# Row maxima of causal scores: diagonal blocks taken by ScalarE and GpSimd instead of a masked pass of VectorE

## The chip, the core and the metric

The kernel runs on one core of a Trainium2 chip. The metric is the device time of one execution in microseconds (us), the median of several runs. Engines are named as in the profile: PE is TensorE (PEld its weight loads), DVE is VectorE, ACT is ScalarE, POOL is GpSimd, SP is SyncE, which only issues DMAs here.

## The reference

One layer of a transformer with modulated norms, for 8 sequences ("batches" below) of 1024 tokens with 256 features, 16 heads of 16 dimensions:

```python
h = _layernorm(x) * (1 + ca) + sa
x = x + ga * attention(h)        # 16 heads, causal, softmax over keys
h = _layernorm(x) * (1 + cb) + sb
x = x + gb * (shared_ffn(h) + routed_ffn(h))   # 8 experts, the top 2 of each token
...
scores = jnp.einsum('...hqd,...hkd->...hqk', q, k) / np.sqrt(d_model)
scores = jnp.where(causal, scores, -1e+30)
attn = jax.nn.softmax(scores, axis=-1)
```

## The kernel before

**Work and stages.** The 16 heads of a batch are taken in four groups of four heads. For each group the kernel first finds, for every query and head, the largest allowed score (the "maxima"). That number goes as two extra rows into the query operand, so that the second computation of the scores, with keys on the partitions, comes out of the matmul with its maximum already taken off, and ACT can apply the exponential as it stands. The maxima of a group are computed one group ahead of their use.

**Slots.** A batch has 80 slots (`SLOTS`), 20 a group (`GROUP`). In slot t PE computes one unit of scores into a bank (`scores`, L1804), ACT takes the exponential of it out of the bank into one of `RING` = 8 probability buffers in SBUF (`exps`, L1076), POOL zeroes the triangle of a unit on the diagonal (`select`, L890), and PE multiplies the probabilities of slot t - 4 (`LAG`) with the values (`values`, L1827). Into the same slots tables of numbers lay the rest of the work: the projections of the next batch (`qk`, `v`, `turn`), and for the batch before it the output projection, the second norm, the router and the shared feed-forward network (`up` L1841, `down` L1893, with ACT's L1098 and L1109, DVE's L1310, L1320 and L1328, POOL's L959). The first batch has instead the splitting of the weights (`share`). After the last batch follow the tiles of the experts.

**Maxima.** In the first 14 slots of a group (`MAX_SLOTS`) PE also computes 18 chunks of scores of the next group: `MAX_CHUNKS` lists nine, and each is done for both pairs of heads (`PAIRS`). A chunk fills one bank, 128 queries by 1024: 512 keys of each of the two heads of a pair (`s`). Its entries `(qt, k0, nk, at)` say which block of 128 queries, which keys, and where in the bank. The two heads lie on different partitions of the operands, so their matmuls (L1780) run beside each other. DVE reads the bank:

```python
if p % NCH not in MASKED:
    vec.tensor_reduce(max_part[:, :, i, col:col + 1].rearrange("p s n -> p (s n)"), of, AX.X, ALU.max).then_inc(max_read, 1)
...
        last = vec.tensor_tensor_reduce(scored, scored, mask[:, 512 - nk:], scale=1.0, scalar=NEG, op0=ALU.add, op1=ALU.max,
                                        accum_out=max_part[:, s, i, to:to + 1])
```

Four of the nine chunks lie wholly below the diagonal or have no piece that ends at it: one reduce (L1273). The five others (`MASKED`) hold a piece that ends with a block on the diagonal, and each of their pieces (eight in all, on two sides) is one instruction that adds the mask and takes the maximum (L1279, in the profile CUSTOM_DVE_ANT_0) and one that reads the accumulator (DVE_READ_ACCUMULATOR2_ANT, L1279 too). `shifts` (L1289 to L1292) then folds the partial maxima, and a turn on PE (`max_turn`, L1791), a copy on ACT (L1059) and two DMAs (L677) bring them into the query operand.

**Banks and order.** PSUM has three banks of 1024 columns (`BUFFERS`) that serve all of this in turn; two further ones take the value products. `WORK` is one list of steps, and every engine goes through it in that order with its own share of each step. Which bank a step takes is planned when the program is built (`buffers`): the one that is free first by the tables `BUSY` and `READ`, with `READ_MASKED` = 20 for a masked chunk and 18 for a plain one. PE waits (`take`, `was_read`) until the last user of that bank has been read. The expert weights of the tail are loaded over the query and key operands and the first probability buffers when these are done (`fetch`, L690).

**At the start** the 18 chunks of group 0 are computed and read one after the other, with nothing else beside them.

Of the kernel before, what the change touches and what calls it, by code (L numbers as in the profile page):

```python
# [14 lines left out]
P = 128  # L15
# [34 lines left out]
RING = 8  # L50
# [6 lines left out]
SEG = {0: 0, 2: 1, 1: 2, 5: 3, 6: 4, 4: 5, 3: 6, 7: 7}  # L57
MAX_CHUNKS = (
    (((3, 0, 512, 0),), 24),
    (((7, 0, 512, 0),), 28),  # L60
    (((7, 512, 512, 0),), 29),
    (((5, 0, 512, 0),), 14),
    (((0, 0, 128, 0), (2, 0, 384, 128)), 3),
    (((6, 0, 512, 0),), 16),
    (((1, 0, 256, 0), (5, 512, 256, 256)), 10),
    (((4, 0, 512, 0),), 21),
    (((6, 512, 384, 0), (4, 512, 128, 384)), 17),
)
NCH = len(MAX_CHUNKS)
MASKED = [i for i, (pieces, _) in enumerate(MAX_CHUNKS) if any(k0 + nk == (qt + 1) * P for qt, k0, nk, _ in pieces)]  # L70
MAXES = PAIRS * NCH

# [167 lines left out]
def work(v):  # L240

    units, tail, spill, head = BODY[v]
    out = []
    for t in range(SLOTS if units else LAG + 2):
# [12 lines left out]
        if not units:  # L257
            continue
        extra = [("normalise", 0)] if t == NORMALISE_AT else []
# [9 lines left out]

        readers = ("rest", "place", "low", "lengths")  # L270
# [66 lines left out]
READ_MASKED = 20  # L337
# [9 lines left out]
def buffers(v, was):  # L347
# [3 lines left out]
    for kind, *at in WORK[v]:  # L351
# [14 lines left out]
        if kind in RINGED and kind not in READER and (kind not in PARTS_OF or at[1] == PARTS_OF[kind] - 1):  # L366
            free[took[use]] = now + (READ_MASKED if kind == "max" and at[1] % NCH in MASKED else READ[kind])
            closed.add(use)
# [15 lines left out]
POOL_SET = 15 + 2 * NE  # L384


def adaln_layer(nc, x, w_qk, w_v, w_o, ffn_w, router_w, bias, c_t, w_mod, out):
# [15 lines left out]
    with ExitStack() as ctx:  # L403
# [9 lines left out]
        arena = sb("arena", [P, 2 * NG * PAIRS * T + RING * 2 * GH * QC], F16)  # L413
# [20 lines left out]
        mask = sb("mask", [P, 512], BF16)  # L434
        ident = sb("ident", [P, P], F32)
        ident_b = sb("ident_b", [P, P], F16)
        max_part = sb("max_part", [P, 2, PAIRS, 4 * NT], F32)
# [37 lines left out]
        probs = flat.rearrange("p (r n) -> p r n", r=RING)  # L475
# [38 lines left out]
        late = flat[:, RING // 2 * GH * QC:]  # L514
# [49 lines left out]
        max_full, max_read, max_ready, max_turned = sem("max_full"), sem("max_read"), sem("max_ready"), sem("max_turned")  # L564
        rows_ready, shift_in = sem("rows_ready"), sem("shift_in")
# [44 lines left out]
        def at_max(b, g, p):  # L610
            return b * (NG * MAXES) + (g * MAXES + p + 1)

# [38 lines left out]
        def _(sp):  # L651
# [31 lines left out]
            def fetch(e):  # L683
# [4 lines left out]
                if g >= NG:  # L688
                    sp.wait_ge(values_done, at_unit(B - 1, SLOTS - 1 - RING // 2))
# [171 lines left out]
        def _(pool):  # L861
            gp = nc.gpsimd
            gp.memset(ident[:, :], 0.0).then_inc(pool_set, 1)
            gp.memset(mask[:, :], 0.0).then_inc(pool_set, 1)
# [1198 lines left out]
```

## Time and profile before

| what | us |
|---|---|
| three runs | 2168.48, 2179.09, 2185.64 |
| median | 2179.09 |
| profiled execution, span from first to last instruction | 2187.9 |

The profiled execution is one of its own, and its span is the only time known of it. Its instructions' durations are what the prediction counts with. The profile page gives busy time by engine; a window of the trace gives the same for a stretch of time; the chain of waits goes back from the last instruction to what released each step.

### The profile page before, as it was taken

How to read it: one execution, taken by the hardware profiler on the slowest of the kernel's cores; microseconds unless marked ns; L12 is line 12 of the kernel's file. 1: busy time of each engine (PE TensorE's matmuls, PEld its weight loads, DVE VectorE, ACT ScalarE, POOL GpSimd, SP SyncE). 2: the span in 40 equal slices, each digit the busy share in tenths (PEclk: the TensorE clock that was granted, in tenths of full speed). 3: DMA queues.
4: the chain of work that ended last, by engine and by line, in shares of the span. 5: the costliest groups of instructions: out<-in, count | busy, mean ns of one | idle time of the engine just before them, and what ended most of it. 6: DMA issues, size and time to landing. Idle time of an engine off the chain costs nothing.

```text
span 2187.9 us, 47736 instructions
## 1 busy us (share of the span) xinstructions
PE 1958.7 (90%) x17942; PEld 1036.3 (47%) x17942; DVE 1634.5 (75%) x4447; ACT 1085.8 (50%) x1417; POOL 830.9 (38%) x825
## 2 busy tenths in 40 slices
PE   5778889899999989999999999999998988999995
PEld 2223334344444444444443434343434577788773
DVE  7887788777877788778878877878787376655575
ACT  1556445554555455545554555455554545444431
POOL 1121133234323432343233333333232357876653
PEclk7688879999999999999999999999998999999998
DMA  3346220201111201120211020211100446797696
GB/s 125 94 169 192 89 64 16 59 22 46 45 38 43 71 20 47 37 70 16 65 30 62 22 65 22 71 30 53 49 26 25 158 88 113 133 170 123 153 285 201
DMA packets 109663, 175.67 MB, mean 80 GB/s; under 512 B 14576, under 2 KB 80376, under 8 KB 108288
## 3 DMA queue, kind: packets, MB, share of 16 engines
q1 hardware_dynamic: 82656, 136.37, 20.9%
q0 software_dynamic: 26592, 36.00, 9.1%
q8 instruction: 149, 2.44, 0.5%
q14 instruction: 74, 0.61, 0.1%
q10 hardware_dynamic: 192, 0.26, 0.1%
HBM read 76.43 MB, written 70.44 MB: 67 GB/s over the span
## 4 chain that ended last, share of the span: by engine, by line
PE 55%; DVE 29%; ACT 5%; issue 4%; DMA 3%; POOL 2%; SPq 2%; POOLq 0%; ACTq 0%; DVEq 0%
PE bank L1841 11%; DVE bank L1279 8%; PE bank L1893 8%; DVE max_part L1273 8%; PE bank L1873 6%; PE bank L1804 5%; PE misc L1827 5%; PE bank L1780 4%; PE pv L1827 3%; PE bank L1754 3%; PE bank L1884 2%; PE bank L1920 2%; ACT arena L1076 2%; PE bank L1742 1%; DVE max_part L1279 1%
## 5 line engine op out<-in xcount | busy, mean ns | idle before, releaser
L1076 ACT ACTIVATE arena<-bank 128x1024 f32<-128x1024 f32 (+1 forms) x640 | 593.2, 935 | 422.7 <-PE bank L1804 419.1
L1279 DVE CUSTOM_DVE_ANT_0 bank<-bank,mask 128x512 f32<-128x512 f32 (+3 forms) x1024 | 472.2, 521 | 65.8 <-PE bank L1780 62.4
L890 POOL TENSOR_SCALAR_AFFINE_SELECT arena<-arena 128x512 f32<-128x512 f32 x256 | 170.3, 672 | 651.0 <-ACT arena L1076 650.4
L1841 PE MATMUL bank<-feat_parts,ffn_sb 128*128 128x512 f16 x1536 | 367.4, 388 | 8.8 <-DVE max_part L1279 4.9
L1273 DVE TENSOR_REDUCE max_part<-bank 128x2 f32<-128x1024 f32 x256 | 312.4, 1220 | 28.2 <-PE bank L1780 26.2
L1804 PE MATMUL bank<-arena 50*128 50x256 f16 (+1 forms) x2560 | 246.3, 272 | 68.7 <-DVE max_part L1273 22.7
L1780 PE MATMUL bank<-arena 48*128 48x512 f16 (+3 forms) x1536 | 234.1, 350 | 56.7 <-DVE max_part L1279 20.8
L953 POOL DMA_INDIRECT sum<-arena,feat x142 | 231.9, 1633 | 138.1 <-issue 67.0
L959 POOL TENSOR_TENSOR hidden<-silu_h,hidden 128x512 f16<-128x512 f32 x128 | 155.8, 1220 | 234.0 <-ACT hidden L1109 233.4
L1827 PE MATMUL misc<-arena,v_sb 128*32 128x256 f32 (+1 forms) x3072 | 239.8, 386 | 1.9 <-POOL arena L890 1.9
L1841 PEld LDWEIGHTS bank<-feat_parts,ffn_sb 128*128 128x128 f16 x1536 | 141.5, 99 | 197.8 <-issue 33.1
L1873 PE MATMUL bank<-parts,arena 128*128 128x256 f16 x1704 | 201.0, 275 | 13.7 <-DVE arena L1493 11.4
L1893 PE MATMUL bank<-ffn_sb,hidden 128*128 128x256 f16 x1536 | 182.4, 276 | 21.7 <-POOL hidden L959 12.5
L1804 PEld LDWEIGHTS bank<-arena 50*128 50x128 f16 x2560 | 82.6, 96 | 246.0 <-issue 82.0
L1873 PEld LDWEIGHTS bank<-parts,arena 128*128 x1704 | 161.8, 98 | 41.1 <-issue 16.3
L1780 PEld LDWEIGHTS bank<-arena 48*128 48x128 f16 x1536 | 60.5, 95 | 245.0 <-issue 95.6
L1893 PEld LDWEIGHTS bank<-ffn_sb,hidden 128*128 128x128 f16 x1536 | 147.2, 99 | 57.1 <-issue 23.5
L1827 PE MATMUL pv<-arena,v_sb 128*32 128x256 f32 (+1 forms) x2048 | 159.2, 385 | 0.0
L1098 ACT ACTIVATE silu_h<-bank 128x512 f32<-128x512 f32 x112 | 66.9, 597 | 162.5 <-PE bank L1841 162.3
L1279 DVE DVE_READ_ACCUMULATOR2_ANT max_part<- 128x1 f32 x1024 | 145.3, 142 | 0.0
L935 POOL DMA_INDIRECT lists<-rows,slot_now x128 | 127.6, 997 | 34.9 <-issue 32.4
L1493 DVE SCALAR_TENSOR_TENSOR arena<-bank,arena 128x512 f32<-128x512 f32 x71 | 49.0, 690 | 119.1 <-ACT arena L1132 119.0
(218 smaller groups left out, 2477.2 us busy)
## 6 DMA issues: line engine op xcount, KB each, us to landing
arena<-parts SPq DMA_DIRECT2D x380, 64.0 KB, 2.3
feat<-lists SPq DMA_DIRECT2D x71, 265.0 KB
sum<-feat_parts SPq DMA_DIRECT2D x9, 1024.0 KB, 6.1
rows<-x SPq DMA_DIRECT2D x8, 1024.0 KB, 5.5
x_sb<-x SPq DMA_DIRECT2D x16, 512.0 KB, 5.6
sum<-norm SPq DMA_DIRECT2D x14, 512.0 KB, 3.3
ffn_parts<-hidden SPq DMA_DIRECT2D x8, 768.0 KB, 4.1
arena<-ffn_parts SPq DMA_DIRECT2D x8, 768.0 KB, 6.7
```

The costliest lines, as they stand in the source:

```text
L890: gp.affine_select(p, p, [[0, GH], [1, P]], ALU.is_ge, 0.0, 0, -1).then_inc(masked, 1)
L953: gp.indirect_dma_start(sum_dram[i % 2], bass.IndirectOffsetOnAxis(ap=tile_id[i % 8][:, t:t + 1], axis=0), tile_out[i % 4][:, t, :], None, ...
L959: gp.tensor_tensor(hidden[:, 1, k % 8, :], silu_h[:, k % 2, :], hidden[:, 0, k % 8, :], ALU.subtract).then_inc(hidden_low, 1)
L1076: sc.activation(to[:, :, lo:QC], of[:, :, lo:QC], ACT.Exp, scale=SCALE / QK_SCALE ** 2).then_inc(exp_done, 1)
L1273: vec.tensor_reduce(max_part[:, :, i, col:col + 1].rearrange("p s n -> p (s n)"), of, AX.X, ALU.max).then_inc(max_read, 1)
L1279: last = vec.tensor_tensor_reduce(scored, scored, mask[:, 512 - nk:], scale=1.0, scalar=NEG, op0=ALU.add, op1=ALU.max, accum_out=max_part[ ...
L1780: last = mm(to[:, 512 * s + at:512 * s + at + nk], q_stack[r, g, i, qt * P:(qt + 1) * P], k_stack[r, g, i, k0:k0 + nk], start=True, stop=True)
L1804: last = mm(to[:, at + lo:at + QC], k_stack[r, g, i, kt * P:(kt + 1) * P], q_stack[r, g, i, QC * c + lo:QC * (c + 1)], start=True, stop=True)
L1827: last = mm(attended[n % 2][32 * j:32 * j + 32, lo:QC], v_sb[:, kt, h:h + 32], probs[:, u % RING, at + lo:at + QC], start=(kt == 0), stop= ...
L1841: last = mm(to[:, 512 * m:512 * m + 512], w_up[s][W_PART[i]][:, f, m * RH + h * P:m * RH + (h + 1) * P], feat_parts[:, A_PART[i], f, c * 5 ...
L1873: last = mm(to[:, 512 * h + ROWS * m:512 * h + ROWS * (m + 1)], weights(W_PART[x] * UW + f * 2 * RH + m * RH + h * P, P), tile_feat[i % 2] ...
L1893: last = mm(to[:, 0:D], hidden[:, A_PART[i], j, t * P:(t + 1) * P], w_down[j // 2][W_PART[i]][:, j % 2, :], start=(i == 0 and j == 0), sto ...
```

## The change

The masked pass is gone. `MAX_CHUNKS` is cut anew: each of the eight diagonal blocks of 128 by 128 is now a piece of its own, and the eight fill two chunks (`DIAG_AT` = 1 and 5 of nine). The seven other chunks need no mask and are read by one DVE reduce each, which gives one partial maximum for each run of 512, 256 or 128 keys (the last number of an entry); `max_part` has five places a query block in place of four (`KEPT`). A diagonal chunk is copied by ACT out of its bank into one of three copy buffers (`copy_max`), masked there by POOL one slot later (`select_max`), and reduced by DVE from SBUF two slots after that (`diag_max`). PE may write the bank again when ACT has copied it. The copy buffers are the last three of the eight probability buffers, of which five are left (`RING` = 5, `ARENA` = 8). In the bank plan a diagonal chunk counts 18 like a plain one. The load of an expert's weights over the probability buffers waits for the last use of just the buffers that it covers.

```diff
-RING = 8
+RING = 5
+ARENA = 8
...
+KEPT = 5
+SEG = {7: 0, 1: 1, 5: 2, 3: 3, 6: 4, 2: 5, 4: 6, 0: 7}
 MAX_CHUNKS = (
-    (((3, 0, 512, 0),), 24),
-    (((7, 0, 512, 0),), 28),
...
+    (((7, 0, 512, 0),), 0, 1, 512),
+    (((7, 896, 128, 0), (5, 640, 128, 128), (6, 768, 128, 256), (4, 512, 128, 384)), 1, 10, 128),
...
+    (((1, 128, 128, 0), (3, 384, 128, 128), (2, 256, 128, 256), (0, 0, 128, 384)), 9, 10, 128),
...
+DIAG_AT = (1, 5)
+OF_DIAG = [p % NCH in DIAG_AT for p in range(MAXES)]
+COPIES = 3
...
+        made[t + 1] += [("select_max", *e[1:]) for e in maxes if OF_DIAG[e[2]]]
+        made[t + 3] += [("diag_max", *e[1:]) for e in maxes if OF_DIAG[e[2]]]
...
-READ_MASKED = 20
+READ_MASKED = 18
...
-                    sp.wait_ge(values_done, at_unit(B - 1, SLOTS - 1 - RING // 2))
+                    used = ((e + 1) * 2 * UW - 2 * NG * PAIRS * T - 1) // (2 * GH * QC)
+                    sp.wait_ge(values_done, at_unit(B - 1, SLOTS - RING + used))
...
+            def select_max(b, g, p):
+                n = at_diag(b, g, p)
+                pool.wait_ge(diag_copied, n)
+                some = copy_of(p).rearrange("p (q n) -> p q n", n=P)
+                gp.affine_select(some, some, [[0, 2 * 4], [-1, P]], ALU.is_ge, NEG, 0, 1).then_inc(diag_masked, 1)
...
+            def copy_max(b, v, g, p):
+                n = at_diag(b, g, p)
+                if past(n - COPIES):
+                    act.wait_ge(diag_read, n - COPIES)
+                act.wait_ge(max_full, at_max(b, g, p))
+                sc.activation(copy_of(p), buffer_of(v, ("max", g, p))[:, :], ACT.Copy).then_inc(diag_copied, 1)
...
+            def kept(g, p, of):
+                pieces, col, step, nk = MAX_CHUNKS[p % NCH]
+                many = sum(x[2] for x in pieces) // nk
+                to = max_part[:, :, p // NCH, col:col + (many - 1) * step + 1:step]
+                return vec.tensor_reduce(to, of, AX.X, ALU.max)
...
+                kept(g, p, buffer_of(v, ("max", g, p))[:, :].rearrange("p (s q n) -> p s q n", s=2, n=nk)).then_inc(max_read, 1)
...
+            def diag_max(b, g, p):
+                dve.wait_ge(diag_masked, at_diag(b, g, p))
+                kept(g, p, copy_of(p).rearrange("p (s q n) -> p s q n", s=2, n=P)[:, :, :, 0:P]).then_inc(diag_read, 1)
...
-                    pe.wait_ge(max_read, at_max(b if at[0] else b + 1, *at))
+                    of = b if at[0] else b + 1
+                    if OF_DIAG[at[1]]:
+                        pe.wait_ge(diag_copied, at_diag(of, *at))
+                    else:
+                        pe.wait_ge(max_read, at_plain(of, *at))
```

The order of DVE's instructions in a group of the loop batch, third to sixth chunk, before (L1279 the masked pass, L1273 the reduce, L1300 and L1302 the normalising of outputs):

```order
L1273 TENSOR_REDUCE max_part<-bank0 128x2
L1279 ISA bank2,max_part<-bank2,mask 128x128
L1279 ISA max_part 128x1
L1279 ISA bank2,max_part<-bank2,mask 128x128
L1279 ISA max_part 128x1
L1279 ISA bank2,max_part<-bank2,mask 128x384
L1279 ISA max_part 128x1
L1279 ISA bank2,max_part<-bank2,mask 128x384
L1279 ISA max_part 128x1
L1300 RECIPROCAL l_inv<-misc 128x8
L1302 TENSOR_TENSOR o_tok<-misc,l_inv 128x2x64
L1273 TENSOR_REDUCE max_part<-bank0 128x2
```

And DVE at the same place after the change (L1312 is `kept`; 128x2x4 are eight partial maxima; arena is a copy buffer; L1351 and L1361 are the silu products):

```order
L1312 TENSOR_REDUCE max_part<-bank1 128x2x4
L1312 TENSOR_REDUCE max_part<-bank0 128x2
L1341 RECIPROCAL l_inv<-misc 128x8
L1343 TENSOR_TENSOR o_tok<-misc,l_inv 128x2x64
L1312 TENSOR_REDUCE max_part<-arena 128x2x4
L1351 SCALAR_TENSOR_TENSOR silu_h<-silu_h,bank0 128x512
L1361 SCALAR_TENSOR_TENSOR silu_h<-bank0,silu_h 128x512
L1312 TENSOR_REDUCE max_part<-bank1 128x2
```

Eight instructions for a chunk with two masked pieces have become one, and the reduce of a copy stands two slots behind the chunk's own place, ahead of that slot's silu products.

ACT at the same place before (L1076 the exponential, of half a unit where it says 4x128; L1066 the copy of an output):

```order
L1076 ACTIVATE arena<-bank0 128x4x128
L1076 ACTIVATE arena<-bank2 128x1024
L1076 ACTIVATE arena<-bank0 128x4x128
L1076 ACTIVATE arena<-bank0 128x1024
L1076 ACTIVATE arena<-bank2 128x1024
L1066 ACTIVATE o_raw<-misc 128x256
L1076 ACTIVATE arena<-bank1 128x1024
L1098 ACTIVATE silu_h<-bank1 128x512
```

And after it (L1112 the exponential, L1087 the copy of a diagonal chunk, L1102 the copy of an output, L1134 the silu's tanh):

```order
L1112 ACTIVATE arena<-bank0 128x4x128
L1087 ACTIVATE arena<-bank2 128x1024
L1112 ACTIVATE arena<-bank1 128x1024
L1112 ACTIVATE arena<-bank2 128x1024
L1102 ACTIVATE o_raw<-misc 128x256
L1112 ACTIVATE arena<-bank2 128x1024
L1087 ACTIVATE arena<-bank1 128x1024
L1134 ACTIVATE silu_h<-bank0 128x512
```

Each copy stands behind its own slot's exponential and ahead of the next one's.

PE in the first slots of such a group before (L1804 scores, L1827 value products, L1780 the chunks):

```order
L1780 MATMUL bank2<-arena 128x512 x2
L1804 MATMUL bank0<-arena 128x256 x4
L1827 MATMUL misc<-arena,v_sb 32x256 x4
L1780 MATMUL bank1<-arena 128x512 x2
L1804 MATMUL bank2<-arena 128x256 x4
L1827 MATMUL misc<-arena,v_sb 32x128 x4
L1780 MATMUL bank0<-arena 128x512 x2
```

And after it (L1855, L1878 and L1831 are the same three):

```order
L1831 MATMUL bank2<-arena 128x128 x8
L1855 MATMUL bank1<-arena 128x256 x4
L1878 MATMUL misc<-arena,v_sb 32x256 x4
L1831 MATMUL bank0<-arena 128x512 x2
L1855 MATMUL bank2<-arena 128x256 x4
L1878 MATMUL misc<-arena,v_sb 32x128 x4
L1831 MATMUL bank1<-arena 128x384 x2
```

The steps of PE keep their order; a diagonal chunk has eight matmuls of 128 columns for two of 512, and the banks fall differently.

## Rows read from the trace of the kernel before

**Rows 1.** Page: busy us by engine; PE in 40 slices, tenths.

```profile
PE 1958.7 (90%) x17942; PEld 1036.3 (47%) x17942; DVE 1634.5 (75%) x4447; ACT 1085.8 (50%) x1417; POOL 830.9 (38%) x825
...
PE   5778889899999989999999999999998988999995
```

**Rows 2.** Windows: length, then busy us of PE, PEld, DVE, ACT, POOL, clock, DMA.

```profile
50.00:260.00 210.00, 164.10 (x1482) 59.47 (x1484) 169.63 (x469) 117.97 (x134) 32.66 (x41) 0.79 0.43 142
1000.00:1213.00 213.00, 198.30 (x1852) 92.51 (x1850) 171.04 (x486) 113.19 (x149) 73.11 (x81) 0.98 0.15 44
```

**Rows 3.** Chain of waits, 1000 to 1213 us: shares by line.

```profile
by line: PE bank L1841 13.8%; PE bank L1893 10.3%; DVE max_part L1273 9.9%; DVE bank L1279 9.2%; PE bank L1804 6.4%; PE misc L1827 5.7%; PE bank L1780 5.1%; PE pv L1827 4.1%; PE bank L1920 3.3%; issue 3.1%; PE bank L1754 2.6%; ACT arena L10
```

**Rows 4.** Windows of stretches with maxima, columns as in rows 2.

```profile
940.00:976.00 36.00, 32.50 (x287) 11.73 (x286) 31.52 (x96) 17.28 (x25) 16.58 (x20) 0.91 0.19 61
1000.00:1029.00 29.00, 25.06 (x257) 11.78 (x254) 26.49 (x81) 17.57 (x22) 10.80 (x13) 1.00 0.01 2
1050.00:1093.00 43.00, 39.98 (x381) 17.41 (x379) 38.49 (x114) 21.56 (x30) 12.13 (x16) 1.00 0.18 47
1049.70:1055.30 5.60, 4.80 (x64) 1.62 (x62) 4.40 (x11) 4.49 (x7) 2.97 (x4) 1.00 0.38 97
```

**Rows 5.** Waits of PE, 1000 to 1213 us: total us, times, longest.

```profile
PE bank L1804 <- DVE silu_h L1320: 2.4, 2, 2.1
PE bank L1804 <- DVE max_part L1273: 2.1, 6, 0.4
PE bank L1893 <- ACT feat L1026: 1.4, 2, 0.8
PE bank L1780 <- DVE max_part L1273: 1.4, 4, 0.5
PE bank L1780 <- ACT arena L1076: 1.3, 4, 0.5
```

**Rows 6.** Same window, L1279 alone, then L1273 alone: DVE busy, clock, DMA.

```profile
1000.00:1213.00 213.00, 61.13 (x256) 0.98 0.15 44
...
1000.00:1213.00 213.00, 39.06 (x32) 0.98 0.15 44
```

**Rows 7.** Groups by form, three reduces of DVE: busy us, mean ns, idle before.

```profile
L1273 DVE TENSOR_REDUCE max_part<-bank 128x2 f32<-128x1024 f32 x256 | 312.4, 1220 | 28.2 <-PE bank L1780 26.2
...
L1484 DVE TENSOR_REDUCE feat<-feat 128x2 f32<-128x16 f32 x71 | 12.1, 170 | 2.4
...
L1289 DVE TENSOR_REDUCE max_row<-max_part 128x32 f32<-128x128 f32 x32 | 8.9, 278 | 0.3
```

**Rows 8.** Timeline of PE: start us, us, line, instruction.

```profile
1043.86 0.62 PE L1791 MATMUL bank<-ident_b,max_bf 128*8 128x128 f16 x8
...
1044.41 0.39 PE L1804 MATMUL bank<-arena 50*128 50x256 f16 x4
...
1050.57 0.39 PE L1780 MATMUL bank<-arena 48*128 48x512 f16 x2
...
1050.80 0.28 PE L1804 MATMUL bank<-arena 50*128 50x128 f16 x4
```

**Rows 9.** ACT's 1024-wide exponential; POOL's select of 512 and 128 elements.

```profile
L1076 ACT ACTIVATE arena<-bank 128x1024 f32<-128x1024 f32 x512 | 520.7, 1020 | 364.7 <-PE bank L1804 361.5 <-PE misc L1827 1.3
...
L890 POOL TENSOR_SCALAR_AFFINE_SELECT arena<-arena x256: 624/634/1981, 68.9 to 1734.5; 128x512 f32<-128x512 f32 x128
...
L880 POOL TENSOR_SCALAR_AFFINE_SELECT ident<-ident 128x128 f32<-128x128 f32 x1 | 0.3, 292 | 0.0
```

**Rows 10.** L1291: min/median/max ns; timeline of it beside POOL.

```profile
L1291 DVE TENSOR_SCALAR max_bf<-max_row x32: 180/182/1924, 61.8 to 1684.6; 128x32 f16<-128x32 f32 x32
...
1037.88 2.36 POOL L965 TENSOR_TENSOR x_sb<-x_sb,gates_sb 128x1024 f32<-128x1024 f32 x1
1038.36 1.92 DVE L1291 TENSOR_SCALAR max_bf<-max_row 128x32 f16<-128x32 f32 x1
```

**Rows 11.** Timeline of SP around the end of the last batch.

```profile
1734.34 2.65 SPq L690 DMA_DIRECT2D arena<-ffn_parts  x4
...
1753.66 5.15 SPq L703 DMA_DIRECT2D feat<-lists  x3
```

More of the change, by code:

```diff
@@ L243, in work @@
     out = []
+    made = [[] for _ in range(SLOTS + 4)]
     for t in range(SLOTS if units else LAG + 2):
@@ L258, in work @@
             continue
+        out += made[t]
         extra = [("normalise", 0)] if t == NORMALISE_AT else []
@@ L366, in buffers @@
         if kind in RINGED and kind not in READER and (kind not in PARTS_OF or at[1] == PARTS_OF[kind] - 1):
-            free[took[use]] = now + (READ_MASKED if kind == "max" and at[1] % NCH in MASKED else READ[kind])
+            free[took[use]] = now + (READ_MASKED if kind == "max" and OF_DIAG[at[1]] else READ[kind])
             closed.add(use)
@@ L383 @@
 DVE_LAST = 104
-POOL_SET = 15 + 2 * NE
+POOL_SET = 13 + 2 * NE
 def adaln_layer(nc, x, w_qk, w_v, w_o, ffn_w, router_w, bias, c_t, w_mod, out):
@@ L611, in at_max, with at_plain, at_diag, copy_of @@
             return b * (NG * MAXES) + (g * MAXES + p + 1)
+        def at_plain(b, g, p):
+            return (b * NG + g) * (MAXES - BLOCKS) + OF_DIAG[:p + 1].count(False)
+        def at_diag(b, g, p):
+            return (b * NG + g) * BLOCKS + OF_DIAG[:p + 1].count(True)
+        def copy_of(p):
+            return blocks[:, (OF_DIAG[:p + 1].count(True) - 1) % COPIES, :]
         def at_up(f, k):
@@ L1009, in _ @@
             gp.memset(zeros, 0.0).then_inc(zeros_made, 1)
+            for p in range(MAXES):
+                if OF_DIAG[p]:
+                    select_max(0, 0, p)
             batch(0, "first")
@@ L1146, in batch @@
                         exps(b, v, at[0])
+                    elif kind == "max" and OF_DIAG[at[1]]:
+                        copy_max(b if at[0] else b + 1, v, *at)
                     elif kind == "raw":
@@ L1194, in _ @@
             part_hi(0, "start", 1)
+            for p in range(MAXES):
+                if OF_DIAG[p]:
+                    copy_max(0, "start", 0, p)
             shift_copy(0, "start", 0)
@@ L1544, in batch @@
                 for kind, *at in WORK[v]:
-                    if kind == "max":
+                    if kind == "max" and not OF_DIAG[at[1]]:
                         maxima(b if at[0] else b + 1, v, *at)
+                    elif kind == "diag_max":
+                        diag_max(b if at[0] else b + 1, *at)
                     elif kind == "shifts":
@@ L1664, in _ @@
             for p in range(MAXES):
-                maxima(0, "start", 0, p)
+                if not OF_DIAG[p]:
+                    maxima(0, "start", 0, p)
+                elif p > DIAG_AT[0]:
+                    diag_max(0, 0, max(q for q in range(p) if OF_DIAG[q]))
+            diag_max(0, 0, max(p for p in range(MAXES) if OF_DIAG[p]))
             shifts(0, 0, 0)
```

53 lines of the change are left out of this document (21 added, 32 removed).

## The prediction

> **What bounds the kernel now.** I read the page first. PE is busy 90% of the span, DVE 75%, and PE's row of slices stands at 8 and 9 from the fourth slice on [rows 1]. That looks like a matmul bound, so the second view is the table of windows: in one loop batch of 213 us PE is busy 198.3 us, DVE 171.0, ACT 113.2, POOL 73.1. The two sides come apart only by what PE doesn't use, 213 - 198.3 = 14.7 us. In the first batch, where the granted clock is 0.79, that is 210 - 164.1 = 45.9 us [rows 2]. The tail with the experts' tiles has no maxima at all. The third view, the chain of waits for the same batch, gives the two lines of the maxima 9.9% and 9.2% [rows 3], which is 19.1% of 213 us, or 40.7 us in which the reader of a bank was what everybody waited for. Cut finer, these 40.7 us lie in stretches where DVE is full: 31.5 of 36 us, 26.5 of 29, 38.5 of 43, and PE idles 3.5, 3.9 and 3.0 us in just these three [rows 4]. So the maxima phases are paced by DVE and by the three banks it holds, and what is left between them by PE. The five largest waits of PE alone in this batch name DVE for 2.4 + 2.1 + 1.4 us and ACT for 1.4 + 1.3 [rows 5]: two thirds DVE.
>
> **What DVE loses.** In one loop batch (four groups of 18 chunks) the masked chunks took 61.13 us in 128 add-and-max instructions and 128 accumulator reads, the plain ones 39.06 us in 32 reduces [rows 6]: 100.2 us, 25.05 a group. After the change each chunk is one reduce of 1024 elements: 14 from a bank and 4 from the copies, 18 a group. The reduce from a bank takes 1.22 us, the one of 16 elements in SBUF 0.170 [rows 7]. That gives (1220 - 170) / 1008 = 1.04 ns an element and 0.15 us fixed. The form that is new is the one with 4 or 8 short pieces in place of 2 long ones. If every piece paid the fixed part, a reduce in eight pieces would cost 1.22 + 6 x 0.15 = 2.1 us, and eight of the 18 are such (with 2 of four pieces beside them): 18 x 1.22 + 8 x 0.9 + 2 x 0.3 = 29.8, more than before. But the reduce of 128 elements in 32 pieces took 0.278 us [rows 7], and the line gives 0.15 + 128 x 1.04 ns = 0.286 for it without any charge for pieces. So I take 1.22 for all, the row nearest in size: 21.96 a group, 3.1 us saved a group, 12.4 a batch. The bounds of the saving are 3.7 (the four reduces of copies without their fixed part) and -4.7 (every piece pays it).
>
> One sentence apart: the table of tiers in "VectorE: DVE Perf Modes" of the Trainium skill has a reduce at 1x from PSUM and from SBUF, so by it nothing is won by reading the copy; no row here has a long reduce from SBUF.
>
> **What of it reaches the end.** 12.4 us a batch are more than PE's waits for DVE, two thirds of 14.7 = 9.8 us. Not all of these go: a bank is still held 1.22 us by each plain chunk, and only the masked ones become shorter (from some 1.5 us for 61.13 / 40 chunks to 1.22 on DVE or 1.02 on ACT). I take two thirds of them, 6.5 us a batch or 1.6 a group. In the first batch PE idles 45.9 us and DVE is full at 169.6 of 210 [rows 2], so there I count the whole 3.1 a group. At the start the 18 chunks of group 0 stand in the chain one behind the other, DVE only; there the saving is about 2 us.
>
> **What PE gains in work.** Two of nine chunks are now four blocks of 128 columns on each side. Per pair 12 pieces become 18; two sides run beside each other, so a group has 12 more steps. Two matmuls of 512 columns begin at 1050.57 and PE begins the next at 1050.80, 0.23 us; eight turns of 128 columns run from 1043.86 to 1044.41, 0.069 us each [rows 8]. A quarter of 0.23 is 0.058, so a cut costs 0.01 to 0.02 us: 0.2 us for the 12 of a group (below: nothing; above: the whole 0.07 each, 0.8 a group).
>
> **What ACT and POOL gain.** 16 copies a batch at 1.02 us, the price of the 1024-wide exponential out of a bank [rows 9]: ACT goes from 113.2 to 129.5 of about 210 us. Each copy stands in ACT's queue in front of the next exponential, which in turn frees a score bank. In short slots this counts: from 1049.7 to 1055.3 ACT was busy 4.49 of 5.60 us [rows 4]. In long slots (an up or down step of 2.7 us) ACT has time. By the third that isn't DVE's, PE waits for ACT up to 4.9 us a batch now; with 15% more load and two copies a group in short slots I take 0.3 us a group (bounds 0 and 4 x 1.02). POOL gets 16 selects a batch. 512 elements take 0.634 us in the middle, 128 take 0.292 [rows 9], so 1024 take 0.63 + 512 x 0.89 ns = 1.09 us, 17 us a batch on an engine that is busy 73 of 213. What they hold up is the next select of probabilities, whose value product comes four slots (some 10 us) later. New is that DVE waits for POOL: behind that wait stand the silu products and further maxima. A copy is made in slot t, masked in t + 1 and read in t + 3, so two slots cover 1.09 us, unless POOL is in x_sb (2.36 us). I count 0.1 us a group.
>
> DVE and POOL do hold each other: the small L1291 takes 0.18 us in the middle, but 1.92 us when it began 0.48 us behind POOL's L965, and both ended within 0.04 us of each other [rows 10]. "SBUF: State Buffer", section "Who interferes with whom", of the Trainium skill says that such a pair of ports is locked for a whole instruction, that a reduce is never part of it, but a DVE instruction with two SBUF inputs is while GpSimd reads SBUF. The trace agrees in this one place. From the rows: if one in ten of the 128 selects catches such an instruction, DVE stands 13 x 1.09 = 14 us in the whole run, of which a half may reach the end. This is inside my range, not in the sum.
>
> **The ring of five.** An exponential of slot t now waits for the values of t - 5. PE issues those in slot t - 1, ahead of the scores that the same exponential waits for anyway. It costs nothing. The loads of the last experts wait for up to three slots more; they went out at 1734.34, and the next load of a tile behind them at 1753.66 [rows 11]; a load of an expert takes less than those 19 us, so there is room for the 2 to 3 us that three slots of values take at this place. If that cover were gone it is at most 3 us, once.
>
> **Sum.** Net a group in the later batches: 1.6 - 0.2 - 0.3 - 0.1 = 1.0; 27 groups (six batches of four and three in the last) give 27 us. First batch: 4 x (3.1 - 0.6) = 10. Start 2. In all 39 us. The profiled span is 2187.9 us and nothing else of that execution is listed; it lies 8.8 us (0.4%) above the median 2179.1 of the runs. 2187.9 - 39 = 2149 for a span, 2179 - 39 = 2140 us for the median.
>
> **Rivals.**
> (a) The saving is hidden. PE is at 198.3 of 213 us, the bank order changed with the new reading times, and ACT takes the place of DVE as the one that holds the banks in the short slots. For it: DVE can catch up in slots with 2.7 us of matmul even today. Against it: DVE is full there too [rows 4]. Only the first batch and the start gain: 10 to 12 us, 2168.
> (b) Slower through ACT. The copies in the first slots of a group stand in front of exponentials that PE waits for. Two of four a group exposed in full and two by half are 3.06 us, with 0.3 for PE and POOL 3.36, against 1.6 saved: 1.76 lost in each of 27 groups, 47 us, less the 12 of the first batch and the start: 35 us, 2214. It decides from the point where over 1.7 us of the 4.1 us of copies a group are exposed (1.6 - 0.3 + 12 / 27). Against it: ACT is busy 53% of a batch, and its idle time before exponentials is the largest on the engine.
> (c) DVE is the only pacer: PE takes up all 3.1 us in each of the 31 groups and 2 at the start: 96 + 2 = 98, 2081. For it: three full stretches with 10.5 us of idle PE. Against it: PE can give back only 14.7 us a batch and waits for ACT too.
> (d) The reduce in pieces is dearer than one in two. Then DVE gains nothing; every group loses up to 4.7 us on DVE, and the time would be above 2250. The row with 32 pieces speaks against it.
>
> **How the numbers follow.** Forecast 0.53, (a) 0.22, (b) 0.12, (c) 0.11, (d) 0.02. A measurement of this kernel tells about 1% (22 us) from no change. Faster by over 1%: 0.53 and 0.11, less 0.02 at the edge, 0.62. Within 1%: (a) and those edges, 0.24. Slower by over 1%: (b) and (d), 0.14. The range reaches from 2098, most of the way to (c), to 2204, most of the way to (b): it leaves out a tenth on each side.
>
> **What would show it.** Per loop batch: DVE's maxima 87 to 90 us in 72 reduces, ACT 129 us, POOL 90, period about 208 to 210 us for 213; the reduces in eight pieces at 1.2 us; the copies at 1.0; DVE's share of the chain's maxima below 17%; PE's waits for ACT's copies and exponentials no more than 1.5 us up. The forecast is wrong if the period is 213 with DVE at 75% (a), if PE's largest wait is for ACT (b), if the period is under 203 (c), or if DVE's busy time in maxima didn't fall (d).

## The result: slower by 2.2%, and the profile after

| | before | after |
|---|---|---|
| median of four runs each, us | 2176.56 | 2224.82 (2223.72 to 2227.45) |
| ratio, 95% interval | | 1.0223 (1.0192 to 1.0254) |
| profiled span, us | 2187.9 | 2222.0 |

The forecast was 2140, the range 2098 to 2204: wrong in sign. The page of after, for comparison with [rows 1]:

```profile
PE 1948.1 (88%) x18710; PEld 1058.2 (48%) x18710; DVE 1557.5 (70%) x2719; ACT 1203.2 (54%) x1545; POOL 963.5 (43%) x951
...
PE   5777789889898989898989898989998988999995
```

DVE lost 77 us, where the forecast's terms come to 98 (3.1 in each of 31 groups and 2 at the start), and PE's nines between the eighth slice and the end of the loop have become eights in every other place. The windows of after, as [rows 2]; the third stretch is the five loop batches:

```profile
50.00:260.00 210.00, 158.21 (x1590) 60.80 (x1590) 153.83 (x195) 134.67 (x153) 52.47 (x60) 0.82 0.43 142
1000.00:1213.00 213.00, 192.12 (x1912) 93.66 (x1910) 155.99 (x259) 125.20 (x162) 89.42 (x96) 0.99 0.15 44
464.00:1559.00 1095.00, 986.54 (x9746) 476.25 (x9740) 806.40 (x1350) 642.97 (x823) 451.44 (x484) 0.99 0.15 42
```

And the same five batches of before:

```profile
461.00:1528.00 1067.00, 992.38 (x9254) 462.27 (x9257) 855.51 (x2430) 567.45 (x741) 368.16 (x404) 0.98 0.15 44
```

28 of the span's 34 us were lost here: a batch takes 219 us where it took 213, and 208 to 210 were forecast. PE's busy time is 6 us lower and the granted clock no worse, so these are waits: PE stands still for 108 us where it was 75. The price of each operation was as forecast, by form (busy us, mean ns, idle before):

```profile
L1312 DVE TENSOR_REDUCE max_part<-bank 128x2 f32<-128x1024 f32 x256 | 312.3, 1220 | 117.8 <-PE bank L1831 115.8
L1312 DVE TENSOR_REDUCE max_part<-bank 128x8 f32<-128x1024 f32 x128 | 155.3, 1213 | 11.9 <-PE bank L1831 11.4
L1312 DVE TENSOR_REDUCE max_part<-arena 128x8 f32<-128x1024 f32 x128 | 154.8, 1210 | 0.0
```

```profile
L1087 ACT ACTIVATE arena<-bank 128x1024 f32<-128x1024 f32 x128 | 131.0, 1024 | 52.4 <-PE bank L1831 52.0
...
L914 POOL TENSOR_SCALAR_AFFINE_SELECT arena<-arena 128x1024 f32<-128x1024 f32 x128 | 139.8, 1092 | 150.0 <-ACT arena L1087 149.9
```

DVE never stood idle ahead of the reduces of copies (0.0), so the masked copies came in time. Yet the chain of waits for 1000 to 1213 us gives the maxima 20.1% where [rows 3] had 19.1:

```profile
by line: DVE max_part L1312 20.1%; PE bank L1892 15.3%; PE bank L1944 10.3%; PE misc L1878 6.6%; PE bank L1855 6.5%; issue 4.9%; PE bank L1971 4.1%; PE bank L1831 3.8%; PE pv L1878 3.1%; ACT arena L1112 1.7%; DVE silu_h L1361 1.6%; DVE silu
```

The engine has less to do and is waited for more. PE's largest waits over the whole span, after (total us, times, longest):

```profile
PE bank L1855 <- DVE max_part L1312: 38.1, 58, 2.5
PE bank L1831 <- DVE max_part L1312: 33.0, 76, 1.3
PE bank L1892 <- DVE max_part L1312: 17.3, 28, 2.4
...
PE bank L1793 <- DVE max_part L1312: 11.2, 16, 0.7
```

and before:

```profile
PE bank L1804 <- DVE max_part L1273: 22.7, 48, 1.3
PE bank L1780 <- DVE max_part L1279: 20.8, 36, 1.9
PE bank L1780 <- DVE max_part L1273: 16.0, 39, 1.4
```

All rows of this view that name the maxima add up to 69.3 us before and 117.9 after; those that name exponentials or copies of ACT fell from 31.0 to 19.8. Two kinds of long step, which PE comes to seldom, now wait for maxima: `up` (L1892, before L1841) 17.3 us where it was 5.5, and the turns of the next batch's rows and of the attention outputs (L1793) 11.2 where it was none. One line's own view counts PE's waits before `up` and those of its weight loads together, which partly run beside each other, so that it is read as a comparison and not as time of PE. Before, then after:

```profile
  ACT arena L1076: 16.5, 51
  DVE max_part L1279: 13.0, 21
  DVE max_part L1273: 2.8, 7
```

```profile
  DVE max_part L1312: 42.2, 63
...
  ACT arena L1112: 5.6, 13
```

Which bank a step takes has changed. Counted in the plans of a loop batch: of the 72 chunks, before, 43 had their bank taken again by the third step behind them and 25 by the fourth; after, 66 by the third and 2 by the fourth. A scores bank went to the second step behind it 31 times before and 8 times after. With all chunks at 18, the planner goes round the three banks in nearly strict turn: 168 of the 198 uses in a loop batch are followed on their bank by the third step behind them, and 123 before. Of the 16 `up` steps 8 take a bank from a chunk, and 4 before.

### The profile page after: what moved, and what is told of

It is laid out like the page before. It is cut to its first block, busy times and chain, and to the rows that moved or that the text cites. A ratio compares the mean times of both kernels' runs of the same rounds, so it can differ in the third digit from the quotient of the medians.

```text
span 2222.0 us, 48054 instructions
## 1 busy us (share of the span) xinstructions
PE 1948.1 (88%) x18710; PEld 1058.2 (48%) x18710; DVE 1557.5 (70%) x2719; ACT 1203.2 (54%) x1545; POOL 963.5 (43%) x951
## 4 chain that ended last, share of the span: by engine, by line
PE 47%; DVE 23%; issue 4%; ACT 4%; POOL 2%; DMA 1%; SPq 1%; POOLq 0%; ACTq 0%; DVEq 0%
DVE max_part L1312 12%; PE bank L1892 11%; PE bank L1944 8%; PE bank L1924 7%; PE misc L1878 4%; PE bank L1855 4%; PE bank L1935 3%; PE bank L1831 2%; PE bank L1971 2%; PE pv L1878 2%; ACT arena L1112 1%; PE bank L1903 1%; DVE stats L1258 1%; DVE silu_h L1361 1%; PE bank L1793 1%
## 5 line engine op out<-in xcount | busy, mean ns | idle before, releaser
L1112 ACT ACTIVATE arena<-bank 128x1024 f32<-128x1024 f32 (+1 forms) x640 | 591.5, 937 | 370.8 <-PE bank L1855 368.9
L1312 DVE TENSOR_REDUCE max_part<-bank 128x2 f32<-128x1024 f32 (+2 forms) x448 | 536.2, 1218 | 149.8 <-PE bank L1831 147.3
L1892 PE MATMUL bank<-feat_parts,ffn_sb 128*128 128x512 f16 x1536 | 363.7, 385 | 19.5 <-DVE max_part L1312 17.3
L1855 PE MATMUL bank<-arena 50*128 50x256 f16 (+1 forms) x2560 | 241.8, 268 | 84.7 <-DVE max_part L1312 38.1
L1831 PE MATMUL bank<-arena 48*128 48x128 f16 (+3 forms) x2304 | 225.5, 286 | 43.4 <-DVE max_part L1312 33.0
L983 POOL TENSOR_TENSOR hidden<-silu_h,hidden 128x512 f16<-128x512 f32 x128 | 155.8, 1220 | 201.8 <-ACT hidden L1145 201.1
L1878 PE MATMUL misc<-arena,v_sb 128*32 128x256 f32 (+1 forms) x3072 | 236.8, 382 | 3.2 <-POOL arena L908 3.2
L1892 PEld LDWEIGHTS bank<-feat_parts,ffn_sb 128*128 128x128 f16 x1536 | 140.6, 99 | 202.8 <-issue 28.5
L914 POOL TENSOR_SCALAR_AFFINE_SELECT arena<-arena 128x1024 f32<-128x1024 f32 x128 | 139.8, 1092 | 150.0 <-ACT arena L1087 149.9
L1855 PEld LDWEIGHTS bank<-arena 50*128 50x128 f16 x2560 | 83.6, 95 | 251.3 <-issue 80.2
L1831 PEld LDWEIGHTS bank<-arena 48*128 48x128 f16 x2304 | 81.0, 96 | 217.7 <-issue 106.7
L1087 ACT ACTIVATE arena<-bank 128x1024 f32<-128x1024 f32 x128 | 131.0, 1024 | 52.4 <-PE bank L1831 52.0
L1878 PE MATMUL pv<-arena,v_sb 128*32 128x256 f32 (+1 forms) x2048 | 155.6, 377 | 0.0
L1312 DVE TENSOR_REDUCE max_part<-arena 128x8 f32<-128x1024 f32 x128 | 154.8, 1210 | 0.0
L1351 DVE SCALAR_TENSOR_TENSOR silu_h<-silu_h,bank 128x512 f32<-128x512 f32 x112 | 76.8, 685 | 95.5 <-ACT silu_h L1134 95.2
```

Source lines behind the costliest of these rows:

```text
L914: gp.affine_select(some, some, [[0, 2 * 4], [-1, P]], ALU.is_ge, NEG, 0, 1).then_inc(diag_masked, 1)
L983: gp.tensor_tensor(hidden[:, 1, k % 8, :], silu_h[:, k % 2, :], hidden[:, 0, k % 8, :], ALU.subtract).then_inc(hidden_low, 1)
L1112: sc.activation(to[:, :, lo:QC], of[:, :, lo:QC], ACT.Exp, scale=SCALE / QK_SCALE ** 2).then_inc(exp_done, 1)
L1312: return vec.tensor_reduce(to, of, AX.X, ALU.max)
L1831: last = mm(to[:, 512 * s + at:512 * s + at + nk], q_stack[r, g, i, qt * P:(qt + 1) * P], k_stack[r, g, i, k0:k0 + nk], start=True, stop=True)
L1855: last = mm(to[:, at + lo:at + QC], k_stack[r, g, i, kt * P:(kt + 1) * P], q_stack[r, g, i, QC * c + lo:QC * (c + 1)], start=True, stop=True)
```

## The experiments

Twelve kernels. The theories: P, the bank plan costs the time; C, ACT's copies do (C', later: a copy costs where its slot is short); M, the short matmul pieces do; D, DVE paces the loop and its savings come back; T, a slot has PE's length and they don't. All numbers are ratios to before, run on the same chip in turn. On these chips (one for r1 to r4, one for r5 to r8, one for r9 to r11, one for r12) before took 2209 to 2222 us, so absolute times of different groups aren't compared. After was not run on them: its 1.0223 was measured where before took 2176.56, and a difference between it and a ratio below is as sure as such ratios carry over from chip to chip. "Before's numbers" of the plan are READ_MASKED = 20 on chunks 0, 2, 4, 6 and 8 of nine.

**r1: no copies.** After, with the diagonal chunks read by DVE out of their banks.

```diff
-OF_DIAG = [p % NCH in DIAG_AT for p in range(MAXES)]
+OF_DIAG = [False for p in range(MAXES)]
```

> The kernel after, but the two diagonal chunks of nine are read by VectorE straight from their banks like the others, without the mask (the causal mask of the diagonal blocks is left out of the maxima): no copy, no select, same bank plan, same matmuls. Theory C (ScalarE's copies make the change slow: they hold the bank and the next exponential): about 2125 to 2150 us, below the kernel before. Theory P (the new bank plan makes it slow) or theory M (the short matmul pieces do): 2200 us or more, as the kernel after.

Measured 1.0153 (1.0099 to 1.0206), span 2240.2. Leaving the copies out seems to give back 0.70 of 2.23 points, but the two intervals overlap; 1.5 points of the loss are there without any copy.

**r2: after with before's plan.** Nothing else differs; the same instructions take other banks.

```diff
-READ_MASKED = 18
+READ_MASKED = 20
+READ_LONG = (0, 2, 4, 6, 8)
...
-            free[took[use]] = now + (READ_MASKED if kind == "max" and OF_DIAG[at[1]] else READ[kind])
+            free[took[use]] = now + (READ_MASKED if kind == "max" and at[1] % NCH in READ_LONG else READ[kind])
```

> The kernel after with the bank plan of the kernel before (chunks 0, 2, 4, 6, 8 of nine planned with 20 for reading, the others with 18). Theory P: back to about 2175 us or below. Theory C or M: within 10 us of the kernel after, 2225.

Measured 0.9985 (0.9964 to 1.0006): the whole loss is gone with before's reading times in the plan. On one chip with r1, r2 is 1.68 points faster although it has the copies and r1 doesn't. The waits before `up` in r2 (L1893), PE and weight loads together:

```profile
  ACT arena L1113: 14.7, 38
  DVE max_part L1313: 9.1, 11
```

9.1 us for 42.2. And its five loop batches, on a chip where those of r4 took 1081:

```profile
452.00:1536.00 1084.00, 991.12 (x9734) 472.26 (x9730) 806.98 (x1350) 642.89 (x820) 450.51 (x483) 0.99 0.15 43
```

**r3: before with the new plan**, READ_MASKED = 18 there.

> The kernel before with the bank plan of the kernel after (every chunk planned with 18). Theory P: 2200 us or more. Theory C or M: within 10 us of the kernel before, 2177.

Measured 1.0511 (1.0454 to 1.0567), the strongest effect of the study, from one number in the old kernel, with before beside it on the same chip. The waits before `up` (L1841), against 13.0 + 2.8 us in the kernel before, and its five batches:

```profile
  DVE max_part L1279: 71.3, 75
...
  DVE max_part L1273: 3.8, 8
```

```profile
489.00:1653.00 1164.00, 1029.11 (x9260) 477.83 (x9254) 860.84 (x2430) 569.10 (x742) 367.44 (x404) 0.95 0.14 40
```

PE is busy 37 us longer here for the same matmuls as before's 992.38: the granted clock is 0.95 for 0.98.

**r4: before with a ring of five**, and the loads' new condition.

> The kernel before with five probability buffers in place of eight, and nothing else. By my working it costs nothing: 2177 us within 5. If the fewer buffers hold exponentials back, 2190 us or more.

Measured 0.9987 (0.9965 to 1.0009): the ring costs nothing. As it is before in all else, its profile (span 2205.8) stands below for before on these chips. Its five loop batches:

```profile
461.00:1542.00 1081.00, 992.58 (x9254) 461.65 (x9250) 855.96 (x2430) 569.67 (x742) 368.68 (x404) 0.98 0.15 43
```

**r5: neither copies nor the new plan**, the edits of r1 and r2 together.

> The kernel after with the bank plan of the kernel before, and the diagonal chunks read by VectorE from their banks without the mask (the causal mask of the diagonal blocks is left out of the maxima): no copy, no select. This is what VectorE's shorter work is worth by itself. If my sum was right in its parts (1.6 us a group, 3.1 in the first batch, less 0.2 for the short matmuls): ratio to before 0.975 to 0.985. If the copies on ScalarE cost nothing, it equals the run with copies and the old plan, 0.9985. If short matmul pieces or chunks cost what was saved, 0.995 or more as well, with ScalarE idle more.

Measured 0.9938 (0.9918 to 0.9959). Against r1 the plan is 2.15 points, against r2 copies and selects are 0.47. What is left is the cheaper reading by DVE, less the short pieces: 0.6%, where my terms for the two come to 39 + 31 x 0.4 = 51 us, 2.3%, and 0.975 to 0.985 was expected.

**r6 and r7: long reading times.** In r6, which is after, a chunk that DVE reads out of its bank counts 21 and a copied one still 18; in r7, which is before, every chunk counts 21.

```diff
-READ = {"scores": 15, "max": 18, "up": 13, "down": 7, "op": 17, "ot": 15, "ln": 15, "router": 6, "turn": 17,
+READ = {"scores": 15, "max": 21, "up": 13, "down": 7, "op": 17, "ot": 15, "ln": 15, "router": 6, "turn": 17,
```

(READ_MASKED is 18 in r6 and 21 in r7.)

> The kernel after, with a plain chunk planned at 21 for reading and a diagonal one at 18. Theory P says that the plan must give a chunk's bank back late, after four uses and not three, and the bank of scores after two: 40 of 72 chunks of a loop batch are at four or more here against 2 (before: 25). Expected ratio 0.980 to 0.998, at or below that of the old plan. If the old plan was good by luck and not by that rule: 1.01 or more.

> The kernel before with every chunk planned at 21 (before: masked 20, plain 18). By the same rule 0.985 to 1.00; if VectorE bounds the maxima whatever the banks do, 1.00; if the rule is wrong, above 1.01.

Measured 1.0008 (0.9992 to 1.0025) and 1.0036 (1.002 to 1.0053), both a little above what I expected (0.980 to 0.998 and 0.985 to 1.00): going further from rotation than before's plan gains nothing. But almost the whole loss is gone in r6, and r7, a table with one kind of chunk only, is far from r3's 1.0511. So it isn't before's particular pattern that matters, but that the plan leaves strict rotation (of r6's 72 chunks 28 are followed on their bank by the fourth step, of r7's 33).

**r8: diagonal chunks filled by wide matmuls** in r2. PE fills the bank by two matmuls of 512 columns with other keys.

```diff
+                if OF_DIAG[p]:
+                    pieces = ((7, 512, 512, 0),)
```

> The kernel after with the old plan, where TensorE fills a diagonal chunk by two matmuls of 512 columns in place of eight of 128 (the chunk then holds other scores: the diagonal blocks are left out of the maxima). Theory M (short pieces cost): by my working 0.2 us a group, 6 us in all, ratio 0.996 against 0.9985; if each piece cost 0.07 us, 25 us, 0.987.

Measured 0.997 (0.9946 to 0.9994), 0.15 points or 3 us under r2, and the intervals overlap. M isn't the cause of the loss.

**r9: copies in adjacent slots** ahead of a long step: r2 with DIAG_AT = (4, 5).

> The kernel after with the old bank plan, and the two diagonal chunks as fifth and sixth of nine in place of second and sixth: their copies then stand in slots 3, 4, 10 and 11 of a group, two of which hold a long step of TensorE, and none in slots 1 and 8, where ScalarE is full. Theory C': what copies cost (0.9985 against 0.9938 without) is paid in the short slots: 0.994 to 0.997. If it is paid anywhere: 0.9985.

Measured 1.0373 (1.0348 to 1.0397), a clear miss: I had taken long slots for good cover. The timeline of r9 where the copies lie (L1088 the copy, L1113 the exponential, L1893 `up`):

```profile
1103.06 1.02 ACT L1088 ACTIVATE arena<-bank 128x1024 f32<-128x1024 f32 x1 [0.28 <-PE bank L1832]
...
1103.98 1.02 ACT L1113 ACTIVATE arena<-bank 128x1024 f32<-128x1024 f32 x1
...
1104.88 1.03 ACT L1088 ACTIVATE arena<-bank 128x1024 f32<-128x1024 f32 x1
...
1105.05 1.90 PE L1893 MATMUL bank<-feat_parts,ffn_sb 128*128 128x512 f16 x8 [0.61 <-ACT arena L1113]
```

The exponential stands behind the first copy, and `up` waits for its bank. The waits before `up` for exponentials have grown to 36.9 us (r2: 14.7), PE and weight loads together:

```profile
  ACT arena L1113: 36.9, 59
  DVE max_part L1313: 12.2, 9
```

This is the smaller part of the 86 us (the 3.88 points over r2). PE alone waited before `up` for exponentials 14.8 us, and 4.1 in r2; at all its steps together it waited for exponentials and copies 49.7 us, and 51.1 in r2, so nothing was lost there in sum. What has grown is the wait for the maxima, before the chunks from 32.1 us in r2 to 55.3, and at all steps from 49.3 to 101.9:

```profile
PE bank L1832 <- DVE max_part L1313: 55.3, 72, 1.6
PE bank L1856 <- DVE max_part L1313: 31.3, 46, 3.8
PE bank L1856 <- DVE silu_h L1362: 23.5, 29, 2.2
```

In all, PE's waits grew by 53 us and its busy time by 37 (1946.5 to 1983.1, at a clock of 0.942 for 0.959), of 88 between the two spans. The plan is r2's, bank for bank. What has changed is that four plain chunks now follow each other at places 0 to 3 and the two diagonal ones at 4 and 5. My reading is that the moments at which banks come free fit that plan less; no run tests it. That copies in long slots are dear isn't shown.

**r10: DVE's reading halved.** r5, in which each reduce reads half of every piece.

```diff
-                kept(g, p, buffer_of(v, ("max", g, p))[:, :].rearrange("p (s q n) -> p s q n", s=2, n=nk)).then_inc(max_read, 1)
+                kept(g, p, buffer_of(v, ("max", g, p))[:, :].rearrange("p (s q n) -> p s q n", s=2, n=nk)[:, :, :, 0:nk // 2]).then_inc(max_read, 1)
```

> As the run without copies under the old plan (ratio 0.9938), but every reduce of the maxima reads half of its elements (the maxima over the other half of the keys of each piece are left out): VectorE works some 37 us less in a loop batch, three times what the change saves. Theory D (VectorE paces the stretches in which it is full, as I had it): 15 us or more a batch, ratio 0.94 or lower. Theory T (those slots have TensorE's length, and VectorE is full of a backlog that costs nothing): at most 4 us a batch, 0.975 to 0.99.

Measured 0.965 (0.9622 to 0.9677). The windows of five batches, r5 and then r10:

```profile
448.00:1532.00 1084.00, 1003.87 (x9738) 475.50 (x9738) 799.97 (x1350) 569.69 (x742) 367.84 (x404) 0.97 0.15 43
```

```profile
420.00:1478.00 1058.00, 997.70 (x9742) 476.42 (x9742) 614.21 (x1350) 567.14 (x742) 367.95 (x404) 0.97 0.15 44
```

DVE did 185.8 us less and 26 came back: 14%. Over the whole run 297 us less (1550.8 to 1253.7) gave 62 us of span, 21%; start, first and second batch give 28 of them. (The two ran on different chips; their ratios differ by 2.88 points, 64 us.) The ratio lies between the two accounts, and so do the 5.2 us a batch: T had set at most 4, D 15 or more. T comes near in the loop, and D holds nowhere in full.

**r11: long steps keep off the chunks' banks.** After, where every step other than scores and chunks sees a bank last used by a chunk as free three units later.

```diff
-            i = min(open_, key=lambda i: (max(free[i], now), free[i], i))
+            late = [free[i] + 3 * (kind not in ("scores", "max") and owner[i] is not None and owner[i][0] == "max") for i in range(BUFFERS)]
+            i = min(open_, key=lambda i: (max(late[i], now), late[i], i))
```

> The kernel after with its own reading times in the plan (18 for every chunk), but a step that is neither scores nor chunk takes a bank last used by a chunk as free 3 units later. If the new plan is slow because up, down and projection steps wait for a chunk's bank: a half or more of the 2.4% comes back, ratio 1.000 to 1.011. If the loss lies with scores and chunks themselves: 1.018 or more.

Measured 1.0127 (1.0094 to 1.016), between what the two accounts gave. The wait before `up` moved instead of going (PE and weight loads together):

```profile
  ACT arena L1113: 42.7, 55
  DVE max_part L1313: 0.9, 2
```

42.2 us for DVE have become 0.9, and 5.6 for the exponential 42.7. 0.96 of the 2.23 points came back. That the long steps stood behind chunks is thus not the whole of the plan's cost. This plan lies between the two others in its rotation as well: 16 of 72 chunks are followed by the fourth step, where after has 2 at 1.0223, r2 25 at 0.9985 and r6 28 at 1.0008. So r11 doesn't separate the long steps from the rotation; what the rest is stays open.

**r12: before without the mask.** The softmax doesn't change if a number larger than the allowed maximum is taken off, so the kernel before, with its own chunks, matmuls, plan and eight buffers, reads each chunk by one reduce over all of it.

```diff
+                nk, many, step = {4: (128, 4, 1), 6: (256, 2, 2), 8: (128, 4, 1)}.get(p % NCH, (512, 1, 1))
+                vec.tensor_reduce(max_part[:, :, i, col:col + (many - 1) * step + 1:step], of.rearrange("p s (q n) -> p s q n", n=nk),
+                                  AX.X, ALU.max).then_inc(max_read, 1)
```

> The kernel before with its own chunks, bank plan and eight buffers, where each chunk is read by one reduce in runs of 512, 256 or 128 keys and the causal mask is left out of the maxima (a softmax shifted by a larger number than its own maximum is the same softmax, so only the shift changes). VectorE's saving without copies, selects or short matmul pieces. From the runs so far: without copies 0.9938, of which short pieces take 0.0015: 0.992. If the layout of the chunks mattered beyond that: below 0.985 or above 0.998.

Measured 0.9856 (0.9813 to 0.9899), faster than the 0.992 that I expected: the fastest of the kernels with DVE's full reading, ahead of before and after. It leaves the masking out of the maxima, so what is subtracted is the largest score of a wider run of keys; that is exact in real arithmetic and safe only where scores above the diagonal don't exceed the allowed ones by more than the exponential's range. Its five loop batches:

```profile
449.00:1522.00 1073.00, 996.50 (x9254) 463.83 (x9250) 799.20 (x1350) 568.44 (x741) 366.91 (x404) 0.98 0.15 43
```

It beats r5 by 0.8 points, of which the short pieces could be some 0.15; the rest wasn't taken apart.

## Why the prediction was wrong, point by point

**The bank plan (no term in the sum).** "The bank order changed with the new reading times" stands only in rival (a), as one reason why a saving might be hidden. Priced there by nothing, it is 2.4 points: 1.0223 to 0.9985 (r2), 2.15 without the copies (r5 and r1), each pair across two chips; and 5.1 in the kernel before on one chip (r3). This is the step that failed. The order of PE quoted ahead of the prediction showed banks falling differently, and I read it as a renaming. The traces show where the time goes. The rows of PE's waits, added up over each span, and PE's busy time (us):

| kernel | plan | waits for maxima | for exponentials and copies | PE busy | span |
|---|---|---|---|---|---|
| before | old | 69.3 | 31.0 | 1958.7 | 2187.9 |
| after | new | 117.9 | 19.8 | 1948.1 | 2222.0 |
| r4 | old | 73.4 | 39.0 | 1951.6 | 2205.8 |
| r3 | new | 160.7 | 14.7 | 1998.4 | 2319.2 |
| r5 | old | 54.6 | 34.9 | 1964.0 | 2195.2 |
| r1 | new | 115.3 | 14.1 | 1960.8 | 2240.2 |
| r2 | old | 49.3 | 51.1 | 1946.5 | 2198.1 |

Each of the pairs r4 and r3, r5 and r1, r2 and after runs the same instructions under the two plans, and PE's wait for maxima doubles or more. Under the old plan the change makes PE wait less for them.

With three banks and PE working in a fixed order, the choice decides which reader each later step stands behind. The new table counts 5 + 18 = 23 units from a chunk's first matmul to the end of its reading and 4 + 15 = 19 for scores, a ratio of 1.21. In the trace of after, from the first matmul of each to the end of its reader, over the five loop batches, a plain chunk took 2.13 us in the mean and scores 1.66: 1.28, nearer the old table's masked chunks (25 / 19 = 1.32). A copied chunk took 1.64, as long as scores. So the new table is the less true one for plain chunks, though the reads have become shorter: a chunk's bank waits in DVE's queue. That this mismatch is why the plan is worse is my reading; the runs show that the plan is.

One place shows the wait. The timeline of after around an `up` (DVE is through with three reduces at 1070.94 + 3.49 = 1074.43, and `up` begins 0.05 us later):

```profile
1070.94 3.49 DVE L1312 TENSOR_REDUCE max_part<-bank 128x2 f32<-128x1024 f32 x3 [1.38 <-PE bank L1831]
...
1072.22 0.39 PE L1831 MATMUL bank<-arena 48*128 48x512 f16 x2 [0.42 <-DVE max_part L1312]
...
1074.48 1.68 PE L1892 MATMUL bank<-feat_parts,ffn_sb 128*128 128x512 f16 x7 [0.38 <-DVE max_part L1312]
```

and of before at the same `up`, which took the bank of an exponential and began while DVE had work from masked passes and a reduce until 1058.96:

```profile
1056.92 2.27 PEld L1841 LDWEIGHTS bank<-feat_parts,ffn_sb 128*128 128x128 f16 x12 [0.23 <-ACT arena L1076]
...
1057.29 0.14 DVE L1279 DVE_READ_ACCUMULATOR2_ANT max_part<- 128x1 f32 x1
...
1057.74 1.22 DVE L1273 TENSOR_REDUCE max_part<-bank 128x2 f32<-128x1024 f32 x1
```

DVE has work queued in both. What differs is who has to wait until it has been worked off.

**"Two thirds of them, 6.5 us a batch".** The saving in the maxima was right: 100.2 us predicted to become 87.8; the 72 reduces of after, with the four of `shifts`, take 86.6 us a batch (a window with the tile max_part alone, DVE and POOL):

```profile
464.00:1559.00 1095.00, 433.23 (x380) 0.00 (x0) 0.99 0.15 42
```

DVE's whole busy time fell by less, 9.8 us a batch in after and 11.2 in r5.

The factor was not right, for two reasons. The 9.8 us a batch that it was taken from were all waits for DVE, and the longest in [rows 5], 2.4 us, is for a silu product that the change leaves alone; in the five loop batches of before PE's waits for the maxima add up to 27.1 us, 5.4 a batch, less than the 6.5 that were to be saved. And most of them don't go. In r5 DVE has 56 us less over five batches than in r4 (855.96 to 799.97), and the period doesn't fall (1081 and 1084 us): PE's waits for maxima fell from 28.8 to 19.2 us and its standing still from 88 to 80, but it was busy 11 us longer at a clock of 0.97 for 0.98. In r12 the period falls by 8 us, 1.6 a batch. In r10 each batch gives back 5.2 of 37.2 us. I had read "DVE is full" in [rows 4] as "DVE paces". As I read it now, a full DVE in a stretch of short slots is a backlog; `up` and `down` steps of 2.8 us let it catch up, and the slots have PE's length as long as the bank that PE wants next is not the one in the backlog.

**"In the first batch I count the whole 3.1 a group".** It went from 171.3 us in r4 to 168.6 in r5 and 165.7 in r12: 2.7 to 5.6 us for a forecast of 12.4, or 10 net (from the first scores of a batch to those of the next). In after it grew, from 175.8 us before to 181.5. The start gained 2.3 (65.9 in r4 to 63.6 in r5); 2 was forecast.

**The reduce in pieces, right.** 1213 ns in eight pieces, 1220 in two. The Trainium skill's table in "VectorE: DVE Perf Modes" has a reduce at 1x from PSUM and from SBUF; the trace agrees with 1213 from a bank and 1210 from a copy. Rival (d) is out.

**"What ACT and POOL gain", right in size.** Copies at 1.02 us, selects at 1.09, as worked out. The sum had 0.4 us a group, 12 in the run; r2 against r5 measured 0.47 points, 10 us. Rival (b) had the sign right, by luck: its mechanism, the copies in front of exponentials, is the small part of the loss, and PE's waits for exponentials and copies fell in after.

**Short pieces and the ring, right.** 6 us forecast, 3 measured (r8), within the error. The ring of five: nothing (r4).

**Ports, not seen as a cost.** L1332, the small instruction of [rows 10] (L1291 there), took 1.9 us five times in 32, where it took over 1.4 us six times before; the selects didn't make more of it:

```profile
L1332 DVE TENSOR_SCALAR max_bf<-max_row x32: 180/181/1895, 58.6 to 1721.0; 128x32 f16<-128x32 f32 x32
```

**The miss in sum.** Forecast -39 us, measured +48 (2224.82 - 2176.56). Of the 87 between them the plan without a term is 2.38 points, 52 us; with the plan put back (r2) the change is worth 0.15 points, 3 us for the 39 forecast, and these 36 are the factor and the first batch. The division rests on r2's ratio holding on the chip of the result.

## What to carry to other kernels

When a change touches a number that a planner reads, the order of resources it hands out is part of the change: compare the two plans first, count who stands behind whom, and time the old plan with the new code and the new plan with the old code before anything is said of the instructions. With few buffers handed out in a fixed order, an engine at nine tenths in a stretch need not pace it; whether it does is seen from the wait of the engine that sets the end, and halving the suspect's work measures its exchange rate directly (here 14 to 21%). A plan that suits one order of the work needn't suit another: r9 kept r2's banks, moved two chunks, and lost 3.9 points.

## What the runs showed of the hardware

**Waits of about 2 us were followed by a lower clock.** In r5 PE stood 2.13 us before scores for a silu product:

```profile
942.70 0.39 PE L1854 MATMUL bank<-arena 50*128 50x256 f16 x4 [2.13 <-DVE silu_h L1361]
```

The matmuls behind it ran at the lower level. The windows of r5 before, in and behind that stretch (columns as in rows 2):

```profile
937.00:943.40 6.40, 4.27 (x39) 1.54 (x39) 5.88 (x19) 2.28 (x4) 0.50 (x3) 1.00 0.00 0
943.40:950.20 6.80, 6.33 (x43) 2.23 (x40) 5.39 (x12) 2.18 (x3) 1.79 (x2) 0.51 0.01 2
950.20:957.00 6.80, 6.45 (x62) 2.27 (x60) 5.50 (x9) 3.93 (x6) 3.65 (x4) 0.99 0.11 40
```

0.51 is the level of 1.2 GHz for 6.8 us: 43 matmuls were begun in it where the next 6.8 us have 62. So a gain in waits can be lost as clock: r5 and r2 have the same 1084 us for five batches, with PE busy 1003.87 at 0.97 in one and 991.12 at 0.99 in the other, for the same matmuls. In r5's five batches each of PE's ten waits of 1.8 to 2.1 us was followed by a stretch at the lower level, 68 us of it in all; r4 has five waits of 2.1 us and 34 us at that level, r3 ten of 2.1 to 2.5 and 120. But r2, with no wait over 1.5 us, has 24 us of it too. In r3 and r9, at 0.95 and 0.96, the clock is a part of the loss. Why one arrangement of waits leads to such a stretch and another doesn't, these runs don't tell.

**A plan's number can cost more than an instruction.** Two units of a table in the kernel before cost 5.1%, over twice what the whole change cost, with every instruction the same.
